# Row ids carried as word 129 of the expert slots' rows, and one scatter in place of two

## The reference

```python
xn = _layernorm(x, axis=-1)
x = x + _L0_attn_ref(xn, ...) + _L0_ffn_ref(xn, Wr, Wg, Wu, Wd)

# _L0_attn_ref: 16 heads of 8, causal, low-rank weights
h = hidden_states + softmax(mask(Q @ K.T)) @ V @ out_U @ out_V + out_b
return h + gelu(layernorm(h) @ fc1_U @ fc1_V + fc1_b) @ fc2_U @ fc2_V + fc2_b

# _L0_ffn_ref: 9 experts of width 352, the best two for each token
topk_w, topk_idx = top_k(softmax(x @ Wr), 2)        # weights normalised to sum 1
out = sum over the two experts e of topk_w * (silu(x @ Wg[e]) * (x @ Wu[e])) @ Wd[e]
```

## Time and profile before

| what | value |
|---|---|
| median of 3 runs | 1439.18 us (1438.09 to 1440.15) |
| span of the profiled execution | 1433.7 us, mean granted TensorE clock 0.822 |
| time of the profiled execution as a run | not given; the median lies 5.5 us above the span |
| PE busy | 1100.7 us (77%), 7814 instructions |
| DVE / ACT / POOL busy | 722.5 / 563.5 / 505.7 us |
| POOL L813 and L815, indirect scatters of attention | 128 each, 976 and 972 ns |
| SP L724, load of a chunk's tokens, 256 KB | 2.8 us from issue to landing |
| POOL L1331, indirect scatters of the experts | 136, 981 ns |

### The profile page before, as it was taken

How to read it: one execution, slowest core, us unless ns; L and a number is a source line. 1 busy time by engine, 2 the same in 40 slices (tenths; PEclk the granted TensorE clock), 3 DMA queues, 4 the chain that set the end, 5 groups by cost and what they waited for, 6 DMA issues and landing times. The chain is left out here.

```text
span 1433.7 us, 29326 instructions
## 1 busy us (share of the span) xinstructions
PE 1100.7 (77%) x7814; PEld 842.6 (59%) x7815; DVE 722.5 (50%) x3240; ACT 563.5 (39%) x1285; POOL 505.7 (35%) x693
## 2 busy tenths in 40 slices
PE   1784495677587687687687669667999999995998
PEld 1772363444354454354455345435999999994987
DVE  6254363454454454455355346353444444444887
ACT  0550152343243243243344235245555555543443
POOL 1024414423422522532531542520555555452110
PEclk9555597886786787787787788778999999997999
DMA  8485413422431431431440432201111111114675
GB/s 261 150 300 145 76 23 68 71 46 49 70 54 40 70 61 33 70 66 28 71 76 18 81 62 40 56 18 30 60 59 60 59 59 59 57 57 134 196 218 166
DMA packets 127273, 118.94 MB, mean 83 GB/s; under 512 B 21513, under 2 KB 102929, under 8 KB 127201
## 3 DMA queue, kind: packets, MB, share of 16 engines
q1 hardware_dynamic: 94560, 64.06, 17.7%
q0 software_dynamic: 21168, 47.35, 14.2%
q10 hardware_dynamic: 11472, 6.75, 1.8%
HBM read 49.29 MB, written 43.13 MB: 64 GB/s over the span
## 5 line engine op out<-in xcount | busy, mean ns | idle before, releaser
L1165 DVE CUSTOM_DVE_ANT_0 att_masked_st<-att_m_ps,att_mask_st 128x128 bf16<-128x128 f32 (+1 forms) x1024 | 312.1, 354 | 335.8 <-remote 157.6
L1070 ACT ACTIVATE att_probs<-att_t_ps 128x512 f32<-128x512 f32 x384 | 227.1, 597 | 480.1 <-remote 233.4
L1331 POOL DMA_INDIRECT y_scratch<-moe_y,moe_row_now x136 | 133.5, 981 | 143.0 <-DVE moe_y L1474 80.8
L809 POOL DMA_DIRECT2D att_k_stack<-att_k_hi x32 | 18.5, 579 | 375.6 <-PE att_t_ps L904 362.7
L813 POOL DMA_INDIRECT slot_x<-att_xn,att_slot_now x128 | 124.9, 976 | 54.0 <-issue 37.0
L815 POOL DMA_INDIRECT slot_row<-att_row_now,att_slot_now x128 | 124.5, 972 | 39.0 <-issue 39.0
L904 PE MATMUL att_t_ps<-att_mask_ts,att_ident_b 128*128 128x256 bf16 (+1 forms) x384 | 138.2, 360 | 0.0
L1468 DVE TENSOR_TENSOR moe_hidden<-moe_gate,moe_up_ps 128x352 f32<-128x352 f32 x136 | 70.8, 521 | 124.4 <-issue 79.8
L1386 PE MATMUL moe_y_ps<-w_down,moe_hidden_t 128*128 (+1 forms) x816 | 113.6, 275 | 2.1 <-DVE moe_y L1474 2.1
L903 PE MATMUL att_t_ps<-att_odd_stack,att_k_stack 97*128 97x512 f32 x192 | 92.2, 481 | 15.7 <-ACT att_probs L1070 10.1
L880 PE MATMUL att_m_ps<-att_k_stack,att_odd_stack 96*128 96x256 f32 x256 | 76.4, 385 | 35.9 <-issue 30.7
(11 more groups left out here) (254 smaller groups left out, 2321.1 us busy)
## 6 DMA issues: line engine op xcount, KB each, us to landing
slot_x<-prep_zeros POOLq DMA_DIRECT2D x17, 512.0 KB, 12.8
moe_x<-slot_x SPq DMA_DIRECT2D x136, 64.0 KB
att_k_stack<-att_k_hi POOLq DMA_DIRECT2D x32, 256.0 KB
mlp_rows<-y_scratch POOLq DMA_DIRECT2D x16, 512.0 KB, 5.0
xn_scratch<-prep_xn SPq DMA_DIRECT2D x16, 256.0 KB, 2.4
xt_scratch<-prep_xt SPq DMA_DIRECT2D x16, 256.0 KB, 2.1
att_xt<-xt_scratch SPq DMA_DIRECT2D x16, 256.0 KB
att_xn<-xn_scratch SPq DMA_DIRECT2D x16, 256.0 KB, 2.8
```

Source lines behind the costliest of these rows:

```text
L1070: act.activation(probs[:, m % PT, :], t_ps[m % 2][:], ACT.Exp).then_inc(exp_done, 1)
L1165: last = dve.tensor_tensor_reduce(out=masked_st[m % 2][:, part], in0=m_ps[m % 2][:, part], in1=mask_st[:, SEQ - width:], scale=1.0, scalar ...
L1331: pool.indirect_dma_start(env["y_dram"][:], bass.IndirectOffsetOnAxis(ap=row_now[c.parity][:], axis=0), y[c.parity][:], None).then_inc(y_s ...
```

## The change

`slot_row` goes. A row of `slot_x` is now 129 words: 128 numbers and the row id. In attention a new pair of buffers `xs` holds two copies of the chunk's tokens, one for each expert, with room for the id in each row; SyncE loads both copies from `xn_scratch` (`load_xs`), GpSimd writes the ids into them, and 8 scatters of 516-byte rows follow each other. The bias addition to `xn` now comes ahead of the scatters and waits for none. In the experts' stage the 129-word tile is loaded into `x`, and GpSimd takes the ids out of the tile itself (`take_row`), two tiles ahead of the scatter that uses them. Since the ids sit in `x`, the load of a new tile into that buffer now waits for this copy too (`row_ready`). The spare rows of `y_scratch` shrink to 1024.

```diff
-    slot_x = nc.dram_tensor("slot_x", [slots, P], F32, kind="Internal").ap()
-    slot_row = nc.dram_tensor("slot_row", [slots, 1], F32, kind="Internal").ap()
+    slot_x = nc.dram_tensor("slot_x", [slots, ROW_WORDS], F32, kind="Internal").ap()
...
+                def load_xs(c, early=False):
+                    if not early:
+                        sp.wait_ge(scattered[c.parity], 16 * 2 * TPC * c.turn)
+                    for k in range(2):
+                        sp.dma_start(xs[c.parity][:, :, k, 0:P], env["xn_tiles"][:, ds(c.index * TPC, TPC), :]).then_inc(xs_loaded[c.parity], 16)
...
                         if not last:
                             load_xn(at(half, d + 1))
+                            load_xs(at(half, d + 1))
...
                 def scatter(c, col):
                     t, k = divmod(col, 2)
                     pool.indirect_dma_start(env["slot_x"][:], bass.IndirectOffsetOnAxis(ap=slot_now[c.parity][:, col:col + 1], axis=0),
-                                            xn[c.parity][:, t, :], None).then_inc(scattered[c.parity], 16)
-                    pool.indirect_dma_start(env["slot_row"][:], bass.IndirectOffsetOnAxis(ap=slot_now[c.parity][:, col:col + 1], axis=0),
-                                            row_now[c.parity][:, col:col + 1], None).then_inc(scattered[c.parity], 16)
+                                            xs[c.parity][:, t, k, :], None).then_inc(scattered[c.parity], 16)
...
+                    pool.wait_ge(xn_loaded[p.parity], 16 * (p.turn + 1))
+                    pool.sem_inc(scatter_started, 1)
+                    pool.tensor_tensor(xn[p.parity][:], xn[p.parity][:], out_bias[:]..., ALU.add).then_inc(x_out_ready, 1)
+                    if not (isinstance(p.index, int) and p.index < 2):
+                        pool.wait_ge(scattered[p.parity], 16 * 2 * TPC * p.turn)
...
                     for col in range(2 * TPC):
                         scatter(p, col)
-                    pool.wait_ge(scattered[p.parity], 16 * 2 * 2 * TPC * (p.turn + 1))
-                    pool.tensor_tensor(xn[p.parity][:], xn[p.parity][:], out_bias[:]..., ALU.add).then_inc(x_out_ready, 1)
...
                         sp.wait_ge(x_turned, c.index - 1)
+                        sp.wait_ge(row_ready, c.index - 1)
                     sp.dma_start(x[c.parity][:], env["slot_x"][ds(c.index * P, P), :]).then_inc(x_loaded[c.parity], 16)
...
+                def take_row(c, d, early=False):
+                    pool.wait_ge(x_loaded[c.parity], 16 * (c.turn + 1))
+                    if not early:
+                        pool.wait_ge(y_stored[c.parity], 16 * (c.turn - 1))
+                    pool.sem_inc(row_started, 1)
+                    pool.tensor_copy(row_now[d % ROWS_AHEAD][:], x[c.parity][:, ROW_AT:ROW_AT + 1].bitcast(U32)).then_inc(row_ready, 1)
...
+                with pool.Fori(1, slot_tiles // ROWS_AHEAD - 1) as quad:
+                    for d in range(ROWS_AHEAD):
+                        take_row(at(2 * quad, d + 2), d + 2)
+                        scatter(at(2 * quad, d), d)
```

More of the change, by code:

```diff
@@ L49 @@
 RANK_QKV, RANK_OUT, RANK_MLP = 48, 96, 64
+ROW_AT, ROW_WORDS = P, P + 1
+FILL = 8
 Step = namedtuple("Step", "index parity turn")
@@ L181, in prepare @@
         v_b = s.sb("v_b", [P, P])
-        zeros = s.sb("zeros", [P, FILL * P])
-        spare_i, spare = s.sb("spare_i", [P, slot_tiles], I32), s.sb("spare", [P, slot_tiles])
+        blank = s.sb("blank", [P, FILL, ROW_WORDS])
         ones = s.sb("ones", [P, P])
@@ L658, in attention @@
         xn = s.two("xn", [P, TPC, P])
+        xs = s.two("xs", [P, TPC, 2, ROW_WORDS])
         slot_now = s.two("slot_now", [P, 2 * TPC], U32)
         row_of = s.sb("row_of", [P, tiles * 2], I32)
-        row_now = s.two("row_now", [P, 2 * TPC])
         q_hi, q_lo, k_hi, k_lo = (s.sb(n, [P, CHUNK], F32R) for n in ("q_hi", "q_lo", "k_hi", "k_lo"))
@@ L847, in _ @@
                 step(chunks // 2 - 1, 1)
+                for k in range(2):
+                    pool.wait_ge(scattered[k], 16 * 2 * TPC * (chunks // 2))
             @block.tensor
@@ L1263, in experts @@
         s = Scope(nc, stack, "moe")
-        x = s.two("x", [P, P])
+        x = s.two("x", [P, ROW_WORDS])
         hi_cols, lo_cols = w_hi.rearrange("p e f -> p (e f)"), w_lo[:].rearrange("p e f -> p (e f)")
@@ L1270, in experts @@
         y = s.two("y", [P, P])
-        row_tiles = [s.sb(f"row_tiles{k}", [n, P]) for k, n in enumerate((P, slot_tiles - P))]
-        row_of = s.sb("row_of", [P, slot_tiles], U32)
-        row_now = s.two("row_now", [P, 1], U32)
+        ROWS_AHEAD = 4
+        row_now = [s.sb(f"row_now{k}", [P, 1], U32) for k in range(ROWS_AHEAD)]
         x_ps = [s.ps(f"x_ps{k}", [P, 512]) for k in range(2)]
@@ L1312, in _ @@
                 load(at(0, 1), True)
-                for k in range(2):
-                    n = row_tiles[k].shape[0]
-                    sp.dma_start(row_tiles[k][:], env["slot_row"][k * P * P:(k * P + n) * P, :].rearrange("(n s) o -> n (s o)", s=P)).then_inc(rows_loaded, 16)
                 with sp.Fori(1, slot_tiles // 2) as half:
@@ L1330, in scatter @@
                     pool.sem_inc(scatter_started, 1)
-                    pool.indirect_dma_start(env["y_dram"][:], bass.IndirectOffsetOnAxis(ap=row_now[c.parity][:], axis=0),
+                    pool.indirect_dma_start(env["y_dram"][:], bass.IndirectOffsetOnAxis(ap=row_now[d % ROWS_AHEAD][:], axis=0),
                                             y[c.parity][:], None).then_inc(y_stored[c.parity], 16)
-                pool.wait_ge(rows_ready, 1)
-                scatter(at(0, 0), True)
-                scatter(at(0, 1), True)
-                with pool.Fori(1, slot_tiles // 2) as half:
-                    scatter(at(half, 0))
-                    scatter(at(half, 1))
+                assert slot_tiles % ROWS_AHEAD == 0
+                take_row(at(0, 0), 0, True)
+                take_row(at(0, 1), 1, True)
+                for d in range(ROWS_AHEAD):
+                    take_row(at(0, d + 2), d + 2, d + 2 < ROWS_AHEAD)
+                    scatter(at(0, d), d)
+                with pool.Fori(1, slot_tiles // ROWS_AHEAD - 1) as quad:
+                    for d in range(ROWS_AHEAD):
+                        take_row(at(2 * quad, d + 2), d + 2)
+                        scatter(at(2 * quad, d), d)
+                quad = slot_tiles // ROWS_AHEAD - 1
+                for d in range(ROWS_AHEAD):
+                    if d + 2 < ROWS_AHEAD:
+                        take_row(at(2 * quad, d + 2), d + 2)
+                    scatter(at(2 * quad, d), d)
                 for k in range(2):
@@ L1348, in turn_x @@
                         pe.wait_ge(x_split, c.index - 1)
-                    pe.transpose(x_ps[c.parity][:, 0:P], x[c.parity][:], ident[:]).then_inc(x_turned, 1)
+                    pe.transpose(x_ps[c.parity][:, 0:P], x[c.parity][:, 0:P], ident[:]).then_inc(x_turned, 1)
                 numbers = []
@@ L1397, in first_step @@
                     turn_hidden(at(0, 0), True)
-                    pe.wait_ge(rows_loaded, 32)
-                    for k, n in enumerate((P, slot_tiles - P)):
-                        last = pe.transpose(y_ps[:, k * P:k * P + n], row_tiles[k][:], ident[0:n, 0:n])
-                    last.then_inc(rows_turned, 1)
                 def step(half, d, left):
```

40 lines of the change are left out of this document (17 added, 23 removed).

## The result

The changed kernel is slower. In the first comparison it took 1488.17 us (median of 4 runs, 1468.43 to 1499.43) against 1438.66 us for the kernel before; the ratio is 1.026 [1.020, 1.032]. Two of the four runs (1491.98 and 1499.43 us) lie over 1.5% above the fastest and are left out of that ratio, which makes the slowdown 38 us. In a later comparison it was 1486.70 us against 1431.78 us, 1.042 [1.034, 1.049], 55 us more. The forecast was 1530 us. Direction and range hold, but the slowdown is 38 to 55 us, and 49 us between the two profiled spans, where 91 were forecast.

The account below looks back on a forecast made before the run. Scatter streams were taken to block attention's engines, TensorE to pace the experts. Span 1433.7 - 107 (attention) + 198 (experts' load chain) = 1525 us, plus 5.5 for the run: 1530 us, range 1400 to 1610.

Parts of the forecast that it names:

- The experts' chain: Experts' stage: tile load waits behind the previous scatter through the ids' copy; 3.70 us a tile, 198 us more.
- the middle of the two ends assumed: Experts' stage: clock expected to go up and down; 198 us taken between ends of 121 and 247 us.
- What blocks in attention: Attention: blocked time follows the length of the scatter stream, with or without stack copies; stream 10.3 us shorter.
- 1.5 was forecast: Attention: scatters start some 1.5 us later because the bias addition now stands ahead of them.
- a us less is worth 0.76 us: Attention: 5.5 of 22.7 blocked us is needed work, so 8.8 us earlier release gives 6.7 us a chunk, 107 us.
- forecast 8.8 us earlier: Attention: release of the blocked engines in each chunk, from a 10.3 us shorter stream starting 1.5 us later.
- The 275 us lost: Attention: 17.2 us lost in each chunk's blocked 22.7 us, over 16 chunks.
- the bound of 233 us: Attention: largest possible gain, ScalarE's remote waits, if single-word scatters alone block and all of it goes.
- rival 1: Attention: single-word scatters alone block and all blocking goes, 233 us gained, total 1404 us; chance 11%.
- The step from span to run: Whole kernel: 5.5 us added to the 1525 us span, the median's distance above the span, making 1530 us.
- Rival 3: Attention gives nothing because the burst of stack copies blocks or starts the blocking; total 1637 us; chance 9%.
- Loads of 256 KB at cost 0: Attention: two new loads a chunk on SyncE are covered, cost 0; without cover 2.8 us a chunk, 45 us.

Follow-up runs that it names:

- before_copy_gate: Kernel before, with SyncE's tile load in the experts' stage also waiting for a small GpSimd copy placed behind each scatter; 1626.81 us, ratio 1.134.
- after_four_x: Changed kernel with four x buffers in the experts' stage in place of two; 1287.34 us, ratio to the kernel before 0.899.
- four_x_sixteen: Changed kernel with four x buffers and each 516-byte row scatter sent a second time, to a tensor nothing reads; 1440.91 us.
- twelve: Kernel before with 12 scatters a chunk: row scatters for the first expert only (4), all 8 single-word ones; 1370.01 us.
- no_scatter: Kernel before with no scatter at all in attention, the bias addition waiting for nothing; 1276.15 us.

## Why the prediction was right or wrong

- **The experts' chain: right.** 3.70 us a tile forecast, 3.64 measured; 198 us forecast, 191.4 measured. The order of GpSimd's list was the cause, as argued: `before_copy_gate` brings the price into the kernel before, `after_four_x` takes it away. At full clock a pair is 7.02 us and not 6.66, since the first link is 0.27 us longer and the load 0.08; the clock fell less (mean 0.93) than the middle of the two ends assumed. The two errors nearly cancel.
- **What blocks in attention: right as far as it went.** Where it occurs, the blocking follows the stream of scatters, whichever kind; `four_x_sixteen` gives the loss back whole. Release came 10.8 us earlier after the first scatter (22.7 - 11.9), about the 10.3 us that the stream got shorter. The first scatter comes 1.2 us later than before (4.15 us behind the start of the K copies in place of 2.9, read from the timelines), which is the bias addition; 1.5 was forecast.
- **The step that failed: "a us less is worth 0.76 us", 107 us.** It measured 141.6 us, 8.9 us a chunk for a release 9.6 us earlier (25.6 us behind the start of the K copies before, 16.0 after): 0.92 us for each. At 0.76 the 9.6 us make 117 us, so 10 of the 35 us that were missing come from the release, forecast 8.8 us earlier, and 25 from the factor. Two things show what the factor left out. First the clock: for the same work TensorE was busy 621.09 us before and 594.75 after. These 26 us are work done faster, at a mean clock of 0.84 in place of 0.77 (some 4 of them may be the 32 matmul records by which the trace after has fewer); not being busy fell by 115 us (241.2 to 126.0), which is near the 107 that I had priced. I had let the clock rise or fall in the experts' sum and left it out of attention's. Second, the price isn't one number: above eight scatters a us of stream costs 0.83 us or more (`twelve`), below eight nothing (`no_scatter`), which fits the stops that are there anyway. I took the mean over a hold that was partly covered.
- **The 275 us lost: read too high.** All sixteen scatters are worth 157 us (862.3 - 705.5). The chunk that I read has a stop of 5 us without them, and in others they cover the stop for the stack copies. So the bound of 233 us, and rival 1's sum with it, was out of reach: taking every scatter away gives 157.
- **The step from span to run:** 5.5 us were added, the median's distance from the span of a profiled run that was itself quicker than the median. A run lies 1.7 us above its own span (1484.37 against 1482.7), which would have made 1526 us.
- **Rival 3** (the stack copies) had a grain of truth that I missed: they make a stop of their own of 7 to 8 us in most chunks, but it is hidden in the kernel before, and so no row there shows it. In the kernel before, a wait of TensorE for the q copies into `att_odd_stack` isn't among its waits at all; it appears where the scatters are taken away.
- **Loads of 256 KB at cost 0, single-word scatters at the row scatters' price: about right.** The loads show no cost (`four_x_sixteen`). Eight single-word scatters leave attention at 725.9 us and eight rows at 700.1; the read-modify-write rule of the Trainium skill (DMA: Bandwidth & Descriptors, Specifications) would make the single words the costlier, and these 26 us, from one profiled run each, are in its direction but small beside the 157 us (862.3 - 705.5) that the stream as a whole was worth.
- **Not foreseen:** that the gain itself hangs on a condition that came and went. The price comes from a chain of waits that has no part in the holding; that it is paid without the holding too is argued, since the changed kernel wasn't run there.

## What to carry to other kernels

When data that another engine reads (here the row ids) moves into a buffer, that buffer is free only when the slowest of its readers is done: follow that reader's list backward for what stands ahead of it, and give the buffer as many copies as that chain is long. Four x buffers in place of two turn 1.026 or more into 0.899 (1.000 where the holding was absent). When a long wait is shortened, ask what it covered (here the stack copies) and how much of the clock comes back with it. And run the kernel before beside every comparison: here it differed by 170 us on one chip within half an hour.

## What the runs showed of the hardware that was not expected

- While GpSimd sends indirect scatters back to back (one in 1.28 us), ScalarE, VectorE and through them TensorE stand from 2 to 5 us into the stream until about 2 us behind it, but for single instructions. Sixteen a chunk cost 157 us of attention against none; single ones 3 to 4.5 us apart cost nothing, nor do 19 us of GpSimd additions.
- This holding came and went: 1441 and 1271 us for one kernel on one chip, over 7 and 29 runs half an hour apart.
- A semaphore that GpSimd raises by a bare increment behind an indirect scatter passed at about the scatter's start, by the 1.84 us from there to the transpose that waited for the load; raised by a copy behind it, it came 1.2 us later. It made 2.85 or 3.65 us a tile.
- Plain transfers of the same pieces hold ScalarE far less (remote waits of 51.2 us in place of 233.4), but other copies land later beside them (TensorE waits 12.3 us in place of 7.1).
- In every second chunk, where the loop goes back, VectorE stands 6.9 to 7.8 us without any scatter, on nothing that the profile shows.
